# Binary FFN weights laid out transposed by the host, and TensorE's transposes of them removed

## What is computed

```
W = base + mean(|w - base|) * sign(w - base)      # for W1, W2, W3 (1792x512, 512x1792, 1792x512)
gate = xn @ W1.T ;  up = xn @ W3.T
ffn = (silu(gate) * up) @ W2.T
```

## Time and profile before

| | us |
|---|---|
| median of the runs | 632.92 |
| lowest, highest (3 runs) | 630.64, 638.28 |
| span of the profiled execution | 632.0 |
| TensorE busy, matmul | 584.8 (93%) |
| VectorE busy | 487.1 (77%) |
| ScalarE busy | 348.1 (55%) |
| GpSimd busy | 157.4 (25%) |

### The profile page before, as it was taken

The page is one execution under the profiler, slowest core; times in us unless marked ns, Lnnn a source line. Parts: engine busy times, 40 slices in busy tenths (PEclk is TensorE's granted clock), DMA queues, the critical chain, the costliest instruction groups (busy, mean ns, idle before and its releaser), DMA issues.

```text
span 632.0 us, 8467 instructions
## 1 busy us (share of the span) xinstructions
PE 584.8 (93%) x2794; PEld 480.9 (76%) x2794; DVE 487.1 (77%) x569; ACT 348.1 (55%) x447; POOL 157.4 (25%) x110
## 2 busy tenths in 40 slices
PE   0698799998999899999999899999999999999993
PEld 0577678886878788888678688888888888888883
DVE  5956776498999999889674488887878888887347
ACT  2547562464655537576443585776848577583210
POOL 3413206543343452210120011011111011111005
PEclk9989899998999999999999999999999999999998
DMA  8798748324333331100730011020111101100303
GB/s 339 305 398 304 200 135 239 114 97 165 100 128 95 95 114 50 51 1 5 158 134 1 0 52 51 11 65 24 50 50 50 50 0 50 50 0 15 118 1 133
DMA packets 56964, 63.09 MB, mean 100 GB/s; under 512 B 15216, under 2 KB 36720, under 8 KB 56944
## 3 DMA queue, kind: packets, MB, share of 16 engines
q1 hardware_dynamic: 56944, 62.84, 30.4%
HBM read 60.73 MB, written 2.10 MB: 99 GB/s over the span
## 4 chain that ended last, share of the span: by engine, by line
PE 71%; DVE 12%; issue 7%; ACT 5%; DMA 2%; POOL 2%; SPq 1%; POOLq 0%; DVEq 0%; ACTq 0%
PE gate_ps L1416 16%; PE up_ps L1416 16%; PE sum_ps L1437 10%; PE tr_ps L1294 5%; PE up_ps L1437 4%; PE gate_ps L1437 4%; PE sum_ps L1590 4%; PE up_ps L1335 3%; DVE weight L1000 3%; PE tr_ps L1398 2%; DVE attn_sum L1040 1%; PE gate_ps L1346 1%; DVE y L923 1%; DMA y<-L_attn_x 1%; ACT ramp L668 1%
## 5 line engine op out<-in xcount | busy, mean ns | idle before, releaser
L1416 PE MATMUL up_ps<-xT,guT 128*128 128x512 f32 x576 | 138.4, 393 | 0.0
L1416 PE MATMUL gate_ps<-xT,guT 128*128 128x512 f32 x576 | 138.4, 393 | 0.0
L1031 DVE SCALAR_TENSOR_TENSOR base<-ramp,base 128x1536 f32<-128x1536 f32 x70 | 122.6, 1752 | 3.6 <-ACT ramp L658 2.1
L1416 PEld LDWEIGHTS up_ps<-xT,guT 128*128 128x128 f32 x576 | 107.0, 188 | 21.5
L1416 PEld LDWEIGHTS gate_ps<-xT,guT 128*128 128x128 f32 x576 | 107.0, 188 | 21.5
L658 ACT ACTIVATE ramp<-raw,ramp_bias 128x1536 f32<-128x1536 int32 x70 | 108.9, 1577 | 0.0
L440 POOL TENSOR_TENSOR weight<-base,scale_trio 128x1536 f32<-128x1536 f32 x14 | 38.7, 2767 | 244.6 <-DVE base L1031 244.6
L1437 PE MATMUL sum_ps<-downT,h_split 128*128 128x512 f32 x288 | 72.1, 400 | 5.1 <-DVE h_split L1021 5.1
L1437 PEld LDWEIGHTS sum_ps<-downT,h_split 128*128 128x128 f32 x288 | 54.3, 192 | 17.3 <-issue 6.4
L627 ACT ACTIVATE guT<-tr_ps 128x512 fp32r<-128x512 f32 x48 | 28.7, 597 | 64.8 <-PE tr_ps L1398 37.2
L639 ACT ACTIVATE h_split<-up_ps 128x512 fp32r<-128x512 f32 x48 | 28.7, 598 | 64.6 <-DVE up_ps L1014 64.6
(11 more groups left out here) (192 smaller groups left out, 798.7 us busy)
## 6 DMA issues: line engine op xcount, KB each, us to landing
raw<-L_ffn_w SPq DMA_DIRECT2D x42, 256.0 KB, 3.6
base<-L_ffn_mean_w SPq DMA_DIRECT2D x42, 256.0 KB, 4.9
scan<-L_ffn_w SPq DMA_DIRECT2D x12, 640.0 KB, 7.8
scan<-L_ffn_mean_w SPq DMA_DIRECT2D x12, 640.0 KB, 8.9
raw<-L_attn_codes_gu SPq DMA_DIRECT2D x14, 512.0 KB, 3.7
attn_codes<-L_attn_codes_attn SPq DMA_DIRECT2D x4, 1024.0 KB, 4.7
raw<-L_attn_codes_down SPq DMA_DIRECT2D x14, 256.0 KB, 3.9
y<-L_attn_x SPq DMA_DIRECT2D x2, 1024.0 KB, 6.5
```

Of the source, the lines that this page charges most:

```text
L1031: nc.vector.scalar_tensor_tensor(base[:, par, :], ramp[:, (step % 2) * TRIO:(step % 2 + 1) * TRIO], NF4_RAMPS[j][2], base[:, par, :], ALU. ...
L1416: last = nc.tensor.matmul(ps, guT[:, par, kind, w_part, hc * P:(hc + 1) * P], xT[:, x_part, hc, th * HALF:(th + 1) * HALF], start=(hc == 0 ...
```

## The change

The host passes two arrays instead of six, `w_laid` and `mean_laid` (3, 128, 14 x 512), in which each chunk of gate, up and down weights already lies as TensorE's products read it. The kernel loads them as they are, with 2 KB for a partition in each 128x512 piece (the down pieces were four of 512 B before), and makes `weight` from them. In block 0 no unit is transposed any more; HI is copied and LO subtracted out of `weight` in SBUF. Waits on `tr_done` become waits on `ffn_weight`, `gate_done`, `up_done`, `down_done` or `w_lo`. `early_high` takes the sign itself out of the difference. Mean, order of chunks, projections, and block 1 stay.

```diff
-    scan_v = [m[FIRST * P:, :].rearrange("(p a) n -> p (a n)", p=P).rearrange("p (k s) -> p k s", s=SCAN)
-              for m in (w1, mean_w1, w3, mean_w3)] + [m[:, :, FIRST * P:] for m in (w2_v, mean_w2_v)]
+    scan_v = [m[kind, :, FIRST * HID:].rearrange("p (k s) -> p k s", s=SCAN)
+              for kind in range(3) for m in (w_laid, mean_laid)]
...
             def load_ffn(c, par):
                 sp.wait_ge(ffn_weight, 3 * c - 3)
-                for dst, gate, up, down in ((raw, w1, w3, w2_v), (base, mean_w1, mean_w3, mean_w2_v)):
-                    sp.dma_start(dst[:, par, 0:HID], gate[ds(c * P, P), :]).then_inc(chunk_loaded[par], 16)
-                    sp.dma_start(dst[:, par, HID:2 * HID], up[ds(c * P, P), :]).then_inc(chunk_loaded[par], 16)
-                    sp.dma_start(dst[:, par, 2 * HID:].rearrange("p (q i) -> p q i", q=HC),
-                                 down[:, :, ds(c * P, P)]).then_inc(chunk_loaded[par], 16)
+                for dst, src in ((raw, w_laid), (base, mean_laid)):
+                    for kind in (GATE, UP, DOWN):
+                        sp.dma_start(dst[:, par, kind * HID:(kind + 1) * HID], src[kind, :, ds(c * HID, HID)]
+                                     ).then_inc(chunk_loaded[par], 16)
...
             def first_high(n):
-                act.wait_ge(tr_done, n + 1)
-                nc.scalar.activation(first_w(n)[:, HI, :], tr_ps[:, n % 2, :], ACT.Copy).then_inc(w_hi, 1)
+                act.wait_ge(ffn_weight, n + 1)
+                if FIRST <= n < 2 * FIRST:
+                    act.wait_ge(gate_done, 2 * (n - FIRST) + 2)
+                nc.scalar.activation(first_w(n)[:, HI, :], weight_s[:, n % SECTIONS, :], ACT.Copy).then_inc(w_hi, 1)
             def early_high():
-                act.wait_ge(tr_done, 1)
-                nc.scalar.activation(signT[:, :], sum_ps[:, 1, :], ACT.Copy).then_inc(sign_T, 1)
-                nc.scalar.activation(first_w(0)[:, HI, :], sum_ps[:, 0, :], ACT.Copy).then_inc(w_hi, 1)
+                nc.scalar.activation(signT[:, :], raw_s[:, 0, :], ACT.Sign).then_inc(sign_T, 1)
+                act.wait_ge(first_loaded[0], 32)
+                nc.scalar.activation(first_w(0)[:, HI, :], base_s[:, 0, :], ACT.Copy).then_inc(w_hi, 1)
...
             def w_high(block_no, c, par, kind):
-                act.wait_ge(tr_done, unit_index(block_no, c, kind) + 1)
+                if block_no == 0:
+                    act.wait_ge(ffn_weight, 3 * c + kind + 1)
+                    if kind == DOWN:
+                        act.wait_ge(down_done, TT * (c // 2 - 1) if isinstance(c, int) else TT // 2 * (c - par) - TT)
+                    else:
+                        act.wait_ge(gate_done if kind == GATE else up_done, 2 * c - 2)
+                    src = weight[:, par, kind * HID:(kind + 1) * HID]
+                else:
+                    act.wait_ge(tr_done, 3 * c + kind + 1)
+                    src = tr_ps[:, (3 * par + kind) % 2, :]
...
             def w_low(block_no, c, par, kind):
-                nc.vector.tensor_tensor(buf[:, LO, :], tr_ps[:, (3 * par + kind) % 2, :],
+                src = weight[:, par, kind * HID:(kind + 1) * HID] if block_no == 0 else tr_ps[:, (3 * par + kind) % 2, :]
+                nc.vector.tensor_tensor(buf[:, LO, :], src,
                                         buf[:, HI, :].bitcast(f32), ALU.subtract).then_inc(w_lo, 1)
...
-                if t == 3:
-                    pe.wait_ge(sign_ready, 1)
-                    transpose4(sum_ps[:, 1, :], lambda q: raw_s[:, 0, q * P:(q + 1) * P])
-                    pe.wait_ge(first_loaded[0], 32)
-                    transpose4(sum_ps[:, 0, :], lambda q: base_s[:, 0, q * P:(q + 1) * P]).then_inc(tr_done, 1)
...
             def unit(block_no, c, par, kind):
+                if block_no == 0:
+                    return
...
-            first_unit(1)
-            first_unit(2)
             first_project(GATE, 1)
-            first_unit(3)
             first_project(GATE, 2)
...
+    def project_tiles(w):
+        return w.reshape(CHUNKS, P, HC, P).transpose(3, 0, 2, 1).reshape(P, CHUNKS * HID)
+    def down_tiles(w):
+        return w.T.reshape(CHUNKS, P, HID).transpose(1, 0, 2).reshape(P, CHUNKS * HID)
```

More of the change, by code:

```diff
@@ L61, in block_kernel @@
                  lora_A_h, lora_A_down, lora_B_attn, lora_B_gu, lora_B_down,
-                 w1, mean_w1, w2, mean_w2, w3, mean_w3, out):
+                 w_laid, mean_laid, out):
     f32, f32r, i32 = mybir.dt.float32, mybir.dt.float32r, mybir.dt.int32
@@ L438, in nf4_scale @@
                 counted(nf4_sum, RAMPS * k + RAMPS)
-                counted(tr_done, 3 * (CHUNKS + k) - 3)
+                if isinstance(k, int) and k < 2:
+                    counted(w_lo, 3 * (CHUNKS + k) - 3)
+                else:
+                    counted(tr_done, 3 * k - 3)
                 nc.gpsimd.tensor_tensor(
@@ L446, in A_down_chunk @@
             def A_down_chunk(k, par):
-                counted(tr_done, 3 * (CHUNKS + k) - 3)
+                if not (isinstance(k, int) and k < 2):
+                    counted(tr_done, 3 * k - 3)
                 nc.gpsimd.tensor_copy(A_down_now[:, par, :], A_down[:, ds(k * P, P)].bitcast(f32)
@@ L1395, in unit @@
                                             start=False, stop=True)
-                elif block_no == 1:
+                else:
                     for n in range(HC):
@@ L1517, in _ @@
                 first_down(t)
-                if t == 3:
-                    unit(0, 4, 0, GATE)
-                if t == 5:
-                    unit(0, 4, 0, UP)
             with pe.Fori(2, 6) as i:
```

74 lines of the change are left out of this document (28 added, 46 removed).

## The result

The changed kernel takes 645.63 us in the median of four runs (644.9 to 646.17), the kernel before 633.1 beside it (630.64 to 638.28): a ratio of 1.0174 with a 95% interval of 1.0118 to 1.023. It is slower by 11 to 12.5 us, though TensorE has 172 matmul instructions less; that it is slower is clear of the noise, whether by more or less than 2% is not. The forecast was 633, with a range of 620 to 644.

A forecast was written before the change was run, and what follows sets the result against it. VectorE, with its waits for GpSimd at the shared SBUF ports, was taken to bound most pairs of block 0. Terms -0.1 +1.1 +0.0 +0.8 -0.7 -0.9 gave +0.2 on a 632.0 span, so 633 us, range 620 to 644.

The forecast's parts named there:

- units: Block 0's groups of four transposes on TensorE: 41 removed at 0.50 us each, 20.5 us, of which little passes through.
- low clock: Before pair 2's downs, TensorE stands about 4 us and starts them at 1.2 of 2.4 GHz: +1.0 us.
- (a): At a pair's end three `w_low` wait for GpSimd's four instructions in a row: +1.3 us in pairs 3 to 5.
- (b): The second chunk's down `w_low`, or the add before it, waits for GpSimd's L433: +1.1 us in pairs 2 to 4.
- meeting with L440: In pair 6 the down `w_low` meets GpSimd's scale L440 (281.19 to 283.96): +1.3 us.
- Gain (c): In pairs 3 to 5, L433 starts 1.5 us earlier through faster loads and holds the attention add less: -1.4 us each.
- Gains where the transposes stood: Waits for TensorE that go: -1.0 in pair 2, -1.0 pair 3 (slow downs), -0.2 pair 4, -0.6 pair 5, -2.2 pair 6.
- The operand at the first downs: The last two `first_low`, now reading SBUF, wait for L433 to about 96.3: +1.4 us (0 to 3.5).
- After block 0: The fold and block 1, which have no edit: 0 us.
- third rival: Port takes more than transposes gave; 3 us each in pairs 2 to 5, 2 at first downs: +14, 647; chance 0.12.
- The signs: Right if pairs 3 and 4 take 37 to 40 us, L1007's maximum is 2 us or more, first projection near 29.
- L433's successor at 6.3 us behind SP: Sign of a right forecast: GpSimd's chunk subtraction L433 starts about 6.3 us behind SP's first issue, before 7.8.

The follow-up runs named there:

- low_psum: The changed kernel, but in block 0 VectorE's LO subtraction reads stale data in PSUM (`tr_ps`) instead of the weights in SBUF; 631.66 us, ratio 0.9959.
- early_split: The kernel before, with only the first gate unit in the new form and GpSimd's subtraction of a chunk cut into three; 634.68 us, ratio 1.0007.
- split3: The changed kernel with GpSimd's subtraction of a chunk cut into three of 128x512; 645.87 us, ratio 1.0184.
- low_early: The changed kernel with HI and LO of the next chunk's gate and up moved from the y adds to mid-pair, down `w_low` earlier; 645.67 us, ratio 1.0167.
- dummy_units: The changed kernel with 41 units of four dummy transposes (of `ident`, into `tr_ps`) put back on TensorE; 647.89 us, ratio 1.0208.
- short_diff: The changed kernel with GpSimd's subtraction of a chunk shortened to 128 of its 1536 columns, so weights not right; 624.91 us, ratio 0.9849.
- short_diff_before: The kernel before with GpSimd's subtraction of a chunk shortened to 128 of its 1536 columns, so weights not right; 625.31 us, ratio 0.9845.
- make_psum: The changed kernel, but VectorE writes its weight combination piece by piece into PSUM (`tr_ps`), from which HI and LO read; 679.38 us, ratio 1.0722.

## Why the prediction was wrong

The picture was right: VectorE bounds most pairs, two SBUF inputs make it wait for GpSimd, and TensorE's 22 us are worth almost nothing. Wrong was the balance. low_psum is the change without the operand's cost, and its trace splits the forecast in two: what the change gives without that cost (the forecast's terms for units, loads and the low clock), and what the operand costs (its terms (a), (b), `first_low` and the meeting with L440). In us, from start of downs to start of downs, each measured number a difference of two profiled executions and so good to a microsecond or two:

| step | without the operand's cost: forecast | low_psum - before | operand's cost: forecast | changed - low_psum | sum: forecast | changed - before |
|---|---|---|---|---|---|---|
| to the first downs | -1.5 | -2.4 | +1.4 | +3.2 | -0.1 | +0.8 |
| pair 2 | 0.0 | +0.7 | +1.1 | +1.3 | +1.1 | +2.0 |
| pair 3 | -2.4 | -0.2 | +2.4 | +1.1 | 0.0 | +0.85 |
| pair 4 | -1.6 | -0.5 | +2.4 | +2.3 | +0.8 | +1.8 |
| pair 5 | -2.0 | -0.85 | +1.3 | +1.8 | -0.7 | +0.9 |
| pair 6 | -2.2 | -1.4 | +1.3 | +3.3 | -0.9 | +2.0 |
| after block 0's last downs | 0 | +3.2 | 0 | +0.9 | 0 | +4.1 |
| all | -9.7 | -1.5 | +9.9 | +13.9 | +0.2 | +12.4 |

So two steps of the forecast failed. The gains that were to pay for the operand, 9.7 us, came to 1.5, and the operand, put at 9.9 us, cost 13.9. The forecast of about nothing was the difference of two sums that were each sized in favour of the change.

- *Gain (c), loads 1.5 us earlier* (-1.4 in each of pairs 3 to 5). The loads were not earlier: a chunk takes 214.37 - 206.43 = 7.9 us from SP's first issue to L409, against 7.8 before. The attention add did lose less (1.76 us against 4.14; over the forty, 50.8 against 55.9), but for another reason: the add of y ahead of it waits 1.27 us for the slow downs (row 192.85), so it starts 2.8 us behind L409 and not 0.4. The wait that is saved is in part spent standing still ahead of it: low_psum's adds take 51.7 us in all, and its pair 3 is 0.2 us shorter than before.
- *Gains where the transposes stood* (-1.0 in pair 2, -1.0 in pair 3 for slow downs, -0.2, -0.6, -2.2). In pairs 5 and 6 low_psum has most of them (-2.2 of -2.8). In pairs 2 and 3 it has next to none, and the slow downs that pair 3 was to be rid of are still there (4.2 to 5.5 us for twelve matmuls at 143.57, 181.64 and 219.18).
- *The operand at the first downs.* The forecast let `first_low` wait to about 96.3, +1.4. It began at 92.29, 0.55 ahead of L409 and 2.4 earlier than before, with the transposes gone; its second instruction waited for all of L409, until 96.8: 4.52 against 1.28, +3.2. The place was right, the size was not.
- *Collision (a)* was as described: three `w_low` take 1.43, 1.81 and 1.20 where they took 0.68 each, 2.4 us more. *Collision (b)*, the down `w_low` against L409, did not come in pair 4: it ran 213.92 to 214.61, just into L409's start, in 0.69 us. In the first `w_low` of chunk 4 (115.97) a collision came in a place that had not been listed, and in pair 6 the operand cost 3.3 us where one meeting at 1.3 was listed.
- *After block 0*, set at 0. The downs from 301.29 take 4.54 us for twelve matmuls where those of before take 2.88: the low clock (granted 0.62 over them, 1.00 before) is 1.7 of the 4.1 us. The other 2.4 (0.6 in the fold, 1.8 in block 1) can't be laid to the change: kernels that have the code of before from there on, and fast downs, take from 339.0 to 342.0 us (early_split), and split3 and low_early, with the change in them, take 339.2. The clock had been expected once, before the downs of pair 2, at +1.0.
- *The number of the third rival*, +14 and 647, is near, and its idea that the port takes more than the transposes gave is what happened. Its conditions did not come: L409 starts 7.9 us behind SP's first issue and not under 7.4, and the pairs lose 0.85 to 2.0 us against before and not 3 each. The slow starts that it named did come. That its number is met within 2 us is luck.
- *The signs.* Pairs 3 and 4 of 37 to 40 us, a `w_low` over 2 us, a first projection near 29 us: the signs that were to show the forecast right came, at 39.16, 39.82, 3.06 and 28.68. They hold for the rival as well and could not tell the two apart. (The first projection starts at 29.89 in dummy_units, with the same code up to there, so its 1.3 us are rough.) The one that differs, L433's successor at 6.3 us behind SP, did not come.

The Trainium skill (SBUF — State Buffer, section "Who interferes with whom") says that such a VectorE instruction and GpSimd's exclude each other, and that one PSUM operand frees it. The rows agree: from PSUM the copy takes 0.69 us at every place (and L996 in low_psum), from SBUF up to 3.06 behind L409. The forecast knew the rule and charged the meetings that stood in the timeline of before. These moved with every microsecond; split3 and low_early, which cut or moved an instruction, changed VectorE's sum of such groups by 1.0 and 0.1 us of 115.

What was not tried: a version that gives GpSimd's subtraction to an engine with time left, to see whether short_diff's 625 us can be had with all of the work done. Nor was low_psum run with the added matmuls, which would tell what the low clock costs where the operand costs nothing.

## What to carry to other kernels

- An operand that moves from PSUM to SBUF can cost more than the work it saves. Count VectorE's instructions with two SBUF inputs and GpSimd's beside them as a whole, and not only the meetings of one timeline: here moving or cutting an instruction (low_early, split3) changed who waits and hardly how much.
- A forecast near zero that is the difference of two sums is only as good as both. Build the kernel that has one sum alone, and look for signs that come out differently under the rival.
- When one edit removes work and moves an operand, build the four corners (work on and off, operand here and there) before reasoning on any row: two kernels gave the 14 and the 2. Two kernels that come out level may each have their own limit, as short_diff and short_diff_before have.
- In an order written by hand, a wait that becomes later holds everything behind it in the queue: one load in the wrong place cost make_psum 22 us.

## What the runs showed of the hardware that was not expected

- The waiting goes both ways, and by whole instructions: a `w_low` of 197.47 waits for the scale that ends at 198.35 and ends 0.55 us later, and GpSimd's next scale, 1.04 us before the change, takes 1.49 behind it. L409 grew from 35.1 to 35.8 us over ten, and a 128x512 piece of it took 1.29 us in the median and up to 2.33 (split3).
- VectorE's subtraction takes the same time from PSUM and from SBUF where it doesn't wait: 682 ns median of twenty against 686 (guT, changed kernel).
- TensorE, after 2.2 to 5.5 us without work, took 4.5 to 5.5 us for twelve 128x512 down matmuls of the changed kernel (granted clock 0.50 to 0.63 over them, so at its lower level, 1.2 of 2.4 GHz, for most or all of the time), and 2.88 us directly behind 14 matmuls that did nothing useful (granted 1.00). The length of the stop alone does not tell which it will be: in the kernel before the downs took 4.54 us after 2.09 us without work (145.25) and 3.03 after 2.14 (221.62), and in low_early 2.98 after 2.42 (304.88).
